# The last tiles' weights kept in SBUF, value products later, norm products and bias on other engines

## The reference

```
x = x + deltanet(layernorm(x))     # recurrent: per head a 16x16 state, 512 steps
x = x + experts(layernorm(x))      # 16 experts of 128 hidden units, 4 chosen for each row, and a shared one
x = x + attention(layernorm(x))    # 16 heads of 16, causal, norms and rotary on q and k
x = x + experts(layernorm(x))      # the same experts again
```

## Time and profile before

| what | value |
|---|---|
| median of 3 runs | 5514.33 us (5511.0 to 5519.31) |
| the profiled execution | 5518.57 us, its span 5517.3 us |
| TensorE products | 3331.9 us busy, 60% |
| VectorE | 4095.3 us, 74% |
| ScalarE | 1938.4 us, 35% |
| GpSimd | 1776.0 us, 32% |
| mean granted TensorE clock | 0.805 |
| moved by DMA | 588 MB, 107 GB/s over the span |

### The profile page before, as it was taken

One profiled execution on the slowest core, in us unless ns is written; L12 is line 12 of the kernel. 1 busy time (PEld: TensorE's weight loads), 2 busy tenths in 40 slices (PEclk: granted clock), 3 DMA queues, 4 the chain that ended last, 5 costly groups with the idle time before them and its releaser, 6 DMA issues.

```text
span 5517.3 us, 71359 instructions
## 1 busy us (share of the span) xinstructions
PE 3331.9 (60%) x20252; PEld 2339.9 (42%) x20252; DVE 4095.3 (74%) x10422; ACT 1938.4 (35%) x4713; POOL 1776.0 (32%) x2760
## 2 busy tenths in 40 slices
PE   6312055374544743245267887886698878887875
PEld 2201033253322532135254655564466545664664
DVE  1899988999889998999645666767566667665533
ACT  3111022142221321023034655564456555554332
POOL 1110012502444124410535143314611353226534
PEclk8655576697666976579678998998899999998997
DMA  1310001263213532146352333421133334333787
GB/s 50 120 42 8 0 17 36 93 178 114 69 54 104 168 106 73 58 149 176 109 177 79 104 111 108 122 89 63 64 102 101 104 111 131 116 100 122 228 274 235
DMA packets 425088, 588.15 MB, mean 107 GB/s; under 512 B 57344, under 2 KB 301184, under 8 KB 424576
## 3 DMA queue, kind: packets, MB, share of 16 engines
q1 hardware_dynamic: 375552, 449.31, 27.0%
q0 software_dynamic: 49152, 134.28, 7.3%
HBM read 374.97 MB, written 208.40 MB: 106 GB/s over the span
## 4 chain that ended last, share of the span: by engine, by line
DVE 44%; PE 29%; issue 10%; POOL 9%; ACT 4%; DMA 3%; SPq 1%; DVEq 0%; ACTq 0%; POOLq 0%
PE psum L1061 5%; DVE rec L1125 5%; DVE rec L1127 5%; DVE skb L1130 5%; DVE rec L1138 4%; DVE rec L1141 4%; POOL xbuck L1708 4%; DVE region L1133 3%; DVE psum L1243 3%; PE psum L917 3%; PE psum L1069 2%; PE psum L969 2%; DVE acc L1410 2%; POOL yg L1718 2%; PE psum L861 2%
## 5 line engine op out<-in xcount | busy, mean ns | idle before, releaser
L1061 PE MATMUL psum<-xgT,w 128*128 128x128 f32 x5296 | 768.0, 291 | 83.6 <-issue 28.9
L1718 POOL DMA_INDIRECT yg<-ybuck,words x512 | 534.6, 1044 | 871.9 <-DMA ybuck<-yrow 517.5
L1061 PEld LDWEIGHTS psum<-xgT,w 128*128 128x128 f32 x5296 | 699.8, 205 | 136.0 <-issue 94.7
L1069 PE MATMUL psum<-w_w2T,hid 128*128 x1324 | 452.7, 426 | 307.7 <-DVE hid L1394 229.5
L1243 DVE CUSTOM_DVE_ANT_0 psum<-psum,xo 128x128 f32<-128x128 f32 (+3 forms) x1024 | 473.6, 518 | 146.5 <-PE psum L938 145.2
L1708 POOL DMA_INDIRECT xbuck<-srow,words x512 | 524.4, 1024 | 152.8 <-issue 124.4
L849 PE MATMUL psum<-w_ident,xn 128*128 128x128 f32 x512 | 108.4, 349 | 759.4 <-ACT xn L1427 749.6
L1555 ACT ACTIVATE region<-psum 128x512 f32<-128x512 f32 (+3 forms) x1024 | 402.7, 438 | 327.8 <-PE psum L957 318.5
L1689 POOL TENSOR_SCALAR_AFFINE_SELECT region<-region 128x128 f32<-128x128 f32 x1024 | 290.5, 299 | 611.0 <-ACT region L1555 597.2
L1590 ACT ACTIVATE xgT<-psum 128x256 f32<-128x256 f32 x662 | 252.8, 382 | 653.8 <-PE psum L1051 652.7
L1079 DVE SCALAR_TENSOR_TENSOR sil<-sil,psum 128x128 f32<-128x128 f32 (+1 forms) x465 | 137.3, 295 | 449.1 <-ACT sil L1599 412.3
(11 more groups left out here) (201 smaller groups left out, 7447.5 us busy)
## 6 DMA issues: line engine op xcount, KB each, us to landing
w<-in_w13T SPq DMA_DIRECT2D x662, 256.0 KB, 3.2
xg<-xbuck SPq DMA_DIRECT2D x662, 128.0 KB, 2.9
ybuck<-yrow SPq DMA_DIRECT2D x662, 128.0 KB
xbuck<-x SPq DMA_DIRECT2D x40, 512.0 KB, 5.3
x_scratch<-res SPq DMA_DIRECT2D x64, 256.0 KB, 2.1
acc<-x_scratch SPq DMA_DIRECT2D x128, 128.0 KB
xbuck<-srow,words POOLq DMA_INDIRECT x512
yg<-ybuck,words POOLq DMA_INDIRECT x512
```

The source lines that it names most:

```text
L1061: o = e.matmul(psum[:, mi, half], w13[I % 3][:, k, half], xgT[I % 2][:, k, :], start=(k == 0), stop=(k == 1), skip_group_check=True)
L1069: o = e.matmul(psum[:, mi, 0:D], hid[hi][:, 0:128], w2T[:, bass.ds(expert.pop(I), 1), :].rearrange("p a b -> p (a b)"), start=True, stop=True)
L1718: e.indirect_dma_start(yg[y % 5], None, ybuck[g % 2][0:TILES_OF[g] * 128, :], bass.IndirectOffsetOnAxis(ap=posu[g % 2][:, J - ROWS0[g], k: ...
```

## The change

- After a set's `p_norm`, `p_scale` does the scaling of keys and values on VectorE in eight pieces of 128x512; the small product of beta and reciprocal moves to VectorE too. GpSimd's part of `p_norm` is gone, and `l_turn` waits for the eight pieces.
- `o_in` is only the load. The bias is added in `o_proj` as a third product, of a row of ones with `boA`; `o_add` waits for the load itself.
- The value products of a key tile come after the score products of two further key tiles, not of one; those of a block's last two come at its end. `P` has 16 buffers of the lengths that are needed, over the place of `qkr`.
- `all_weights`, after the last attention block, loads the first weights of all 16 experts, 4 MB in four transfers, where queries and keys lay. Tiles from the eleventh after the last one whose weights were loaded on (`resident`) take them from there: no `t_weight`, the tile's rows are the stationary operand, and the weights move, two products of 256 columns. The hidden values then come out with rows on partitions, so `t_flip` transposes them on TensorE and `t_flipped` copies them on ScalarE, a step before `t_down`, and everything behind it is one step later.
- The last group's tiles use SiLU and one product on VectorE instead of tanh and two.

```
+            for i in range(8):
+                yield LIGHT
+                put("p_scale", k, i)
...
-                        if a == 3 and kt:
-                            put("w_pv", k, kt - 1)
                         yield
+                    ready.append((k, kt))
+                    if len(ready) > 2:
+                        yield from values()
...
+            while ready:
+                yield
+                yield from values()
...
+    put("all_weights")
+    resident[0] = loaded[0] + AHEAD
     while not all(t.done for t in streams):
         advance()
...
+    P = [part((10240, 12288, 13824, 14848)[kt] + a * n, [n]) for kt, n in enumerate((512, 384, 256, 128)) for a in range(4)]
...
+                e.matmul(psum[:, mi, 256:512], ones[:, :], boA[0:1, :], start=False, stop=True).then_inc(s["ow"], 1)
...
+                if kept:
+                    pe.wait_ge(s["d_all"], 64)
+                    pe.wait_ge(s[mf[0]], mf[1])
+                    up = w13all[:, bass.ds(expert[I], 1), :, :].rearrange("p a k m -> p (a k) m")
+                    for k in range(2):
+                        o = e.matmul(psum[:, mi, 0:256], xgT[I % 2][:, k, :], up[:, k, :], start=(k == 0), stop=(k == 1))
...
+            elif name == "t_flip":
...
+                e.transpose(psum[:, mi, 0:128], hid[hi][:, 0:128], ident[:, :]).then_inc(s["fl"], 1)
...
+            elif name == "p_scale":
+                k, i = u
+                four, f = slice(i // 2 * 4, i // 2 * 4 + 4), flat2[k % 2][:, 1 - i % 2, :]
+                st = stage[k % 2][:, 2 * (i % 2), four, :]
+                dv.wait_ge(s["brec"], 2 * k + 2)
+                e.tensor_tensor(st, st, bc(f, 1, 4), ALU.mult).then_inc(s["bnorm"], 1)
...
+                ac.wait_ge(s["pv"], 64 * (i // 4))
                 e.activation(qkr[i % 4], bank_of(mi), ACT.Copy).then_inc(s["qkc"], 1)
...
-                if I < TILE0[GROUP_OF[TANH]]:
+                if I < TILE0[GROUP_OF[TANH]] or I >= TILE0[NG - 1]:
...
-                e.tensor_tensor(st[:, 0, :, :], st[:, 0, :, :], bc(f[:, 1, :], 1, 16), ALU.mult).then_inc(s["bpool"], 1)
-                e.tensor_tensor(st[:, 2, :, :], st[:, 2, :, :], bc(f[:, 0, :], 1, 16), ALU.mult).then_inc(s["bpool"], 1)
...
-                e.tensor_tensor(xo[oi], xo[oi], boA[:, :], ALU.add).then_inc(s["rb"], 1)
...
+            elif name == "all_weights":
+                sp.wait_ge(s["pv"], 64 * NB)
+                for i in range(0, NE, 4):
+                    e.dma_start(w13all[:, i:i + 4, :, :], T["w13T"][:, i:i + 4, :, :]).then_inc(s["d_all"], 16)
```

More of the change, by code:

```diff
@@ L225, in first_rows @@
             nth[f"xo{oi}"] += 16
-            nth["rows"] += 1
-            r = nth["rows"]
-            put("o_in", r, q, n, j, oi, of, nth[f"xo{oi}"])
+            v = nth[f"xo{oi}"]
+            put("o_in", q, n, j, oi, of)
             mi, mf = yield from misc.take()
@@ L312, in attention @@
             yield 1
-        turning, closing, out, weighed = [], [], set(), set()
+        turning, out, weighed = [], set(), set()
         def largest():
@@ L373, in weigh, with values @@
                 weighed.add(hg)
[L374 to L382, removed]
+            while ready:
+                yield
+                yield from values()
+        ready = []
+        def values():
+            k, kt = ready.pop(0)
+            put("w_pv", k, kt)
+            if kt == NQ - 1:
+                yield
+                put("w_out", k)
         heads_of, weights = Strand(largest()), Strand(weigh())
-        while not (heads_of.done and weights.done and all(t.done for t in closing)):
-            for t in closing + [weights] + turning + [heads_of]:
+        while not (heads_of.done and weights.done):
+            for t in [weights] + turning + [heads_of]:
                 t.step()
@@ L503, in heads @@
                 put("second_fill")
+    resident, loaded = [TILE0[NG]], [0]
     def tiles():
@@ L509, in tiles @@
             n, bank, hidden = TILES_OF[g], {}, {}
-            for i in range(n + 8):
+            for i in range(n + 9):
                 I = TILE0[g] + i
                 on = lambda lag: 0 <= i - lag < n
+                own = lambda lag: on(lag) and I - lag < resident[0]
+                kept = lambda lag: on(lag) and I - lag >= resident[0]
                 if on(5):
@@ L515, in tiles @@
                     misc.give(bank[I - 5], "xe", I - 4)
-                if on(8):
-                    put("t_out", g, I - 8, bank[I - 8])
-                    misc.give(bank[I - 8], "yo", I - 7)
+                if kept(8):
+                    f = I - 8 - resident[0]
+                    put("t_flipped", f, bank[I - 8])
+                    misc.give(bank[I - 8], "fd", f + 1)
+                if own(8) or kept(9):
+                    o = I - 8 if own(8) else I - 9
+                    put("t_out", g, o, bank[o])
+                    misc.give(bank[o], "yo", o + 1)
                 if on(6):
                     bank[I - 6], mf = yield from misc.take()
-                    put("t_up", I - 6, bank[I - 6], mf)
+                    put("t_up", I - 6, bank[I - 6], mf, kept(6))
                 yield 0.5
@@ L530, in tiles @@
                     put("t_in", g, I)
-                if on(3):
+                if own(3):
                     put("t_weight", g, I - 3)
-                if on(7):
+                    loaded[0] = I - 3
+                if kept(7):
                     bank[I - 7], mf = yield from misc.take()
-                    put("t_down", I - 7, hidden[I - 7], bank[I - 7], mf)
+                    put("t_flip", I - 7, I - 7 - resident[0], hidden[I - 7], bank[I - 7], mf)
+                    hid.give(hidden[I - 7], "fl", I - 6 - resident[0])
+                if kept(8):
+                    bank[I - 8], mf = yield from misc.take()
+                    put("t_down", I - 8, None, bank[I - 8], mf, I - 8 - resident[0])
+                if own(7):
+                    bank[I - 7], mf = yield from misc.take()
+                    put("t_down", I - 7, hidden[I - 7], bank[I - 7], mf, None)
                     hid.give(hidden[I - 7], "f2", I - 6)
@@ L772, in build @@
     maskw = xo[0].bitcast(BF)
+    w13all = part(0, [NE, 2, 2 * INTER])
+    hidT = [part(8192 + i * 128, [128]) for i in range(2)]
     srow, yrow, acc = ([sb(f"{n}{i}", [128, D])[:, :] for i in range(2)] for n in ("srow", "yrow", "acc"))
@@ L821, in build @@
     order = stages()
+    flips = sum(1 for stage in order if stage[0] == "t_flip")
     s = Sems(nc)
@@ L969, in tensor @@
                     o = e.matmul(psum[32 * a:32 * a + 32, 6, kt * 128:SEQ], vb[:, kt, k % 4 * 4 + a, :],
[L970 removed]
+                                 P[w % 16][:, 0:n], start=(kt == 0), stop=(kt == NQ - 1), skip_group_check=True)
                     o.then_inc(s["pv"], 1)
```

61 lines of the change are left out of this document (34 added, 27 removed).

## The result

The changed kernel takes **5421.5 us** (median; 5420.9 to 5424.1) against 5516.8 for the kernel before on the same chip: a ratio of 0.9827, 95% interval 0.981 to 0.9844, or 95 us less. Forecast were 108 less, 5406, with a range from 5350 to 5463. The profiled execution took 5424.1 us.

The account below looks back on a forecast made before the run. VectorE was taken to bound the recurrence, TensorE attention, and DMA the tail by busy share, though weight-load latency held its tiles. Gains of 3.4, 15, 11, 4, 50 and 25 made 108: 5514.3 to 5406 us, range 5350 to 5463.

Parts of the forecast that it names:

- edit 3: Attention: value products two key tiles later cover waits for GpSimd's causal selects; 50 us gained, ends 10 and 90.
- edit 2: Output bias moved from GpSimd's add to a third matmul; 11 us gained from VectorE's lock, 4 from its waits.
- edit 1: Recurrence: norm products move to VectorE, ending its lock by GpSimd; six sets, 15 us gained, ends 10 and 20.
- Start, -3.4: Ahead of the recurrence: the second set's norm products finish sooner on VectorE; 3.4 us gained, ends 0 and 4.5.
- The lock's term: Recurrence: VectorE no longer held under about half of 64 GpSimd bias adds; 11 us gained, ends 0 and 24.
- The waits' term: VectorE's output adds wait less for the bias add; 4 us gained, ends -8 and 15; L1171's waits under 20.
- the first rival: Attention: select waits move to exponentials or maxima, or GpSimd's bursts outlast the cover; 5 instead of 50 us, chance 0.18.
- Edit 4: Tail: resident expert weights, with moving weights and a flip; 25 us gained, ends a 10 us loss and 45 gained.
- (a): Tail's start: four 1 MB loads on SyncE's queue delay the first tile; 4.5 us lost, ends 0 and 14.
- (b): Tail, 54 tiles: without weight loads the pace falls from 2.05 to 1.75 us a tile; 16.5 us gained.
- (c): Tail's gather rows and last tiles: 8 us and 6 us gained, 1.2 lost to the last tile's flip.
- Slower, by the clock: Tail: more transposes halve TensorE's clock, 3.24 us a tile, 5558 us in all; a rival with chance 0.04.

Follow-up runs that it names:

- e2: Kernel before with only the output bias moved from GpSimd's add to a third matmul on TensorE; ratio 1.0 (0.9987 to 1.0014).
- empty step: Kernel before with one empty step more at the end of each group of tiles; ratio 0.9965, attention 2242.9 us.
- e1: Kernel before with only the norm products moved from GpSimd to VectorE in eight pieces; ratio 0.9963, 20 us less.
- e3: Kernel before with only the later value products and 16 score buffers; ratio 0.995, 27 us less, attention 2216.8 us.
- e8: Changed kernel with the four 1 MB weight loads issued after the last score product, ahead of the last value products and output rows; ratio 0.9812.
- e7: Changed kernel with resident weights stationary again, no flip or added copy, every tile reading expert 0's weights; ratio 0.9829.
- e4: Kernel before with only the resident weights, flip, longer tile loop and last group's SiLU; ratio 0.9922, 43 us less.
- e9: Kernel before with GpSimd's two 128x2048 norm products cut into eight of 128x512, still on GpSimd; ratio 0.9991.

## Why the prediction was right, and where it was not

The sum was right for the sign and within 13 us, and parts of it were right only together. With the means above: recurrence -25 (2508.6 to 2483.6), transition +9 (223.9, the six kernels without edits 1 and 2, to 232.5), attention -46, tail -26, start 0: -88, where the median says -95 (-86 to -105 by the interval). That the total came so near is in part luck: two terms that were too big (13 us for edit 3, some 15 for edit 2 by e2's ratio) were largely made up for by the empty step's 10 us in attention, which was in no term, and by edit 1, where e1 shows 5 more than its 15.

**Start, -3.4.** Mechanism right, size under what can be seen. From the reciprocal to the first step it is 17.4 instead of 19.2 us (16.3 to 17.4 in seven kernels with edit 1, 18.2 to 19.8 in seven without), so some 2 us. The sign named for it, a first step near 154, could not be read: it came at 159.4, and at 149.6 to 163.7 us in kernels with the same code up to it.

**Edit 1, -15.** Right: 21 by e1, with a spread of some 7, and 15 by the instructions. Before, 12 of VectorE's instructions in the recurrence ran over 2 us beyond their line's median, 46.2 us in all; in the changed kernel none does, and its longest VectorE instruction there takes 1.03 us. With the shorter excesses the loss was 8.05 us a set on average (48.3 in six) and not the 7.6 of the one set that was worked out; the pieces cost 5.55 a set (33.3 in six) and not 5.1. Had it cost 31 us, as two engines free of each other would have it, e1 would have been slower.

**Edit 2, -11 and -4.** The lock's term was nearly right: the excesses of 0.2 to 2 us of the recurrence's own lines fall from 16.2 us to 7.7 in e2 (7.8 in the changed kernel), 8.5 instead of 11. The waits' term was wrong. The 24.3 us of the earlier trace rows are those of 54 of L1171's 64 adds; the other ten write from another buffer, and with them the line waits 29.7 us. This did not fall under 20, it became 42.6 in this line's rows of the changed kernel,

```profile
  PE psum L929: 35.0, 18
  DMA xo<-in_x: 4.8, 4
  DMA region<-in_x: 2.8, 1
```

and 9 of the 13 us more stand behind the last step, where the transition grew by 6 to 10. The step that failed is "0.43 us at the full clock" for a product that stands where TensorE runs at 0.70: it took 0.89 us there (e2), which the prediction's own 417 ns an instruction, at two instructions a product, could have told, and the added matmuls filled a stretch that had been half free.

**Edit 3, -50.** Attention gave 46, but only 37 of that is this edit's. The waits at the value products fell by 33 us (109.5 to 77.0 in e3), not by 60: some 50 were to be left, under 60 at most, and 63.4 are left in the changed kernel. That the blocks with scatters come near 60 us held (52.0 to 58.6 us in six, 67.7 in one, where it had been 61.6 to 72.8). The step that failed is the cover, 2.9 us for every wait. In the blocks with scatters GpSimd's backlog is carried to the end of the block, where nothing is left to put between: in blocks 2, 6, 10 and 14 it took some 6 us from the last exponential to the last value product and takes 11 to 13, 22 us more in all. The sum had put only some 26 us at the ends of all blocks. A part of the waits also moved, as the first rival has it: 12 us more for the row maxima in e3 (35.0 to 47.0).

**Edit 4, -25.** Gave 26 as a sum of other parts. (a) +10.2 instead of +4.5, with 5 to 7 of it the queue by e8; e7 gets as much of it back without touching the queue, so how the 10 us come about stays open. (b) 21.7 instead of 16.5, as the pace was 1.63 and not 1.75: address arithmetic, flip and ScalarE's copy together cost 0.03 us a tile in a full pipeline (1.60 in e7). (c) 13.1 instead of 12.8. 112 tiles took the resident weights, and not 113. What the prediction did not see is the empty step: 10 us less in attention, 6 to 9 more in the tail. It was read as a change of the last group alone.

**Slower, by the clock.** The granted clock was 1.00 in 5165 to 5253 us of the changed kernel, with three transposes among nine instructions of each tile. The Trainium skill, "TensorE: Matmul & The Clock Gate", Part 4 (PE-mode transpose), does not count these as activity the way matmuls are. No run here took the matmuls away, so the rule itself is neither shown nor refuted; the fall of the clock that was the rival did not come.

**Edit 5, 0.** Not seen by itself; e4 has it and leaves nothing to explain.

## What to carry to other kernels

Read each part of a change for what it does to the order of everything behind it: here one empty loop step moved 10 us in a stage that the edit did not touch, and made a term that was 13 us too big look nearly exact. A wait that is covered by reordering is only gone if the engine that is late catches up before the block ends; look at the ends. Work moved to an engine with free time has to be priced at that engine's clock in the place where it lands.

## What the runs showed of the hardware

GpSimd and VectorE stop each other for single instructions: in e9 pieces of 128x512 on GpSimd follow each other every 1.22 us alone and every 1.56 beside the recurrence, and VectorE's two-input instructions of that shape take 1.63 instead of 0.69, while its one-input reductions keep their 0.67 us.

The start of the same code varied by 14 us, and TensorE's granted clock differed in it. In the earliest (e7, first step at 149.6) and the latest (e8, at 163.7) the same stretch reads:

```profile
100.00:120.00 20.00, 20.00 (x55) 8.23 (x53) 0.00 (x0) 7.81 (x19) 0.00 (x0) 1.00 0.00 1
```

```profile
100.00:120.00 20.00, 20.00 (x39) 8.25 (x38) 0.00 (x0) 6.28 (x15) 0.00 (x0) 0.66 0.00 0
```

TensorE is busy all of it in both, and runs 55 instructions at a clock of 1.00 and 39 at 0.66. What decides when the clock rises isn't settled.

A chip can be 2% slower for the whole program (5627 and 5629 us against 5517 to 5526 for the kernel before) with the recurrence unchanged (2506.6 in e9). There a time carried over from another chip means nothing, and a ratio to the kernel before can be read only with care, as the stages don't slow down alike.
